# State-space phase with 1024-column scans and the step-times-B product of five of 16 states made on ScalarE

## Chip, core and metric

The kernel runs on one core of a Trainium2 chip. The metric is the device time of one launch in microseconds (us); lower is better. The engines are TensorE (PE, with its weight loads PEld), VectorE (DVE), ScalarE (ACT), GpSimd (POOL) and SyncE (SP, which here only issues DMAs).

## What is computed

Eight sequences of 512 tokens of width 128 pass through two blocks, each as `x = x + layernorm(block(layernorm(x)))`. The first block is a state-space layer (Mamba) in both directions, the second an attention and expert layer, which the change doesn't touch. Of the first block, for each direction (256 inner channels, 16 states):

```python
u = silu(conv(x @ Win_u) + convb)          # 4 taps, per channel
dtr, B, C = split(u @ Wx)                  # 8, 16 and 16 wide
dt = softplus(dtr @ Wdt + bdt)
def step(h, (dt_t, u_t, B_t, C_t)):        # over the 512 tokens
    h = exp(dt_t * A) * h + (dt_t * u_t) * B_t
    return h, sum_over_states(h * C_t)
y = (ys + u * D) * silu(x @ Win_z)
return y @ Wout                            # both directions and x are added
```

## The kernel before, in words

`mamba_phase` runs 16 units, one for each batch b and direction d, in the order (0,0), (0,1), (1,0) and so on. Channels lie on the partitions, in two halves h of 128; time lies along the columns. A unit has 32 steps s, one for each state n = s // 2 and half h = s % 2. In each step:

- ACT makes `da = exp(dt * A[n])` (`act_da`), 512 columns, up to 8 steps ahead of the scan that frees the buffer.
- PE broadcasts row n of B to all partitions with a 512-column bf16 product against a selection matrix (`pe_b`, L319), once for each state, into a PSUM bank.
- DVE multiplies it by `dtu = dt * u` (`dve_dbu`, L603) into another PSUM bank and runs the recurrence as one instruction (`dve_scan`, L610, a TENSOR_TENSOR_SCAN). It issues two products, then two scans.
- POOL multiplies the result by C[n], which lies broadcast in SBUF (`pool_hc`, L731).
- PE transposes each 128-column piece of that and adds it in PSUM (`pe_y`, L331), so that y is summed over the states with time on the partitions. It runs LAG_Y = 5 steps behind. The D term comes in the same way from `ud = u * D`, which ACT makes.

Beside the steps of one unit stands the preparation of the next, the *front*: layer norm (DVE, POOL), transposes `pe_xt` and copies `act_xpad` (only for direction 0), eight taps of the convolution `pe_u`, `act_silu_u`, `pe_z`, `act_silu_z`, then the table load back to exp and ln, `pe_xd`, `act_xd`, the split of B into three bf16 parts (`pool_rem`, `pool_part`), `pe_dt`, the softplus in four ACT steps a half (`act_soft`), `dve_dt`. And the *tail* of the unit before: `dve_yg`, `pe_ygt`, `act_ygt`, and behind direction 1 also `pe_out`, the second norm `dve_end` and `pool_x1`. PSUM is full: `bp` 2 banks, `dbu` 2, `yp` 2, `wp` 2; front and tail share `wp`.

The order of every engine's instructions is written out by hand: each of `pe_unit`, `act_unit`, `dve_unit` and `pool_unit` loops over the steps and says at which step of the current unit each piece of front or tail is issued. Each engine takes its instructions in that order, and a wait on a semaphore holds everything behind it. In the kernel before, PE issues the taps at s = 12 to 18, z at 19 and 20, xd at 21 and dt at 24 and 25; ACT issues silu and table load at s = 25, the xd copies at 27 and 30, the softplus at 31; DVE issues dt and dtu after scans 29 and 30, and res, the first step of `dve_end`, after scan 14. SP loads C for a whole unit with two broadcasts, of 1 and 3 MB, into a buffer with a place for each direction, and x right behind it.

## Time and profile before

| | us |
|---|---|
| median of 3 runs | 2225.64 (2219.59 to 2229.83) |
| the profiled execution, its own time | 2225.48 |
| its span, first to last instruction | 2223.7 |
| state-space phase within the span | about 0 to 1050 |

| engine | busy us (share of the span) |
|---|---|
| PE | 1614.2 (73%) |
| DVE | 1626.8 (73%) |
| ACT | 1174.6 (53%) |
| POOL | 1233.7 (55%) |

Busy time is the union of an engine's instructions; neighbours on one engine can overlap by a little, so the distance from start to start is the price of one in a dense stream, and the mean duration is somewhat more. The share over the whole span is a mean over two phases with different limits; the phase from 42 us (first unit) to about 1031 us (last scan) is the one that the change touches. A "granted clock" of 0.50 is TensorE at 1.2 GHz, 1.00 at 2.4 GHz.

### The profile page before, as it was taken

Reading aid. Unit: us, or ns where it says so; the run is one execution under the profiler, and the core shown is the slowest. Engines: PE = TensorE matmul, PEld = TensorE weight load, DVE = VectorE, ACT = ScalarE, POOL = GpSimd, SP = SyncE. Lnnn points to the kernel's source line nnn. Section 1 sums busy time; section 2 is a strip of 40 time slices with the busy share of each in tenths; the row PEclk is TensorE's granted clock in tenths of the full one; section 3 lists DMA queues with packets and bytes.
Section 4 is the critical chain, followed back from the end, with each engine's and each line's share of the span. In section 5 each row is a group of like instructions: output and inputs, shape, how many; then the busy total and the mean of one; then the engine's idle time right before and its main releaser. Section 6 shows DMA issues by size and latency. Waiting matters only on the chain.

```text
span 2223.7 us, 29267 instructions
## 1 busy us (share of the span) xinstructions
PE 1614.2 (73%) x7664; PEld 938.7 (42%) x7664; DVE 1626.8 (73%) x2538; ACT 1174.6 (53%) x1906; POOL 1233.7 (55%) x1097
## 2 busy tenths in 40 slices
PE   3677676766677666765376887877879888897888
PEld 1445454544455444544133343443434434343443
DVE  3999999999999999996262738456384654837455
ACT  4565555656565555561146391754727357282751
POOL 2777677777777677774336280643717346181541
PEclk8888777877888777775567598898989989899999
DMA  4212022121212011120301000000100001000000
GB/s 149 82 77 84 21 82 81 76 95 76 95 76 91 21 74 81 76 91 12 115 6 36 11 27 11 16 35 16 36 8 9 34 16 36 16 10 26 11 0 15
DMA packets 39620, 107.23 MB, mean 48 GB/s; under 512 B 4128, under 2 KB 30048, under 8 KB 34368
## 3 DMA queue, kind: packets, MB, share of 16 engines
q1 hardware_dynamic: 39520, 106.24, 12.6%
q14 instruction: 80, 0.66, 0.1%
q8 instruction: 20, 0.33, 0.1%
HBM read 92.99 MB, written 8.65 MB: 46 GB/s over the span
## 4 chain that ended last, share of the span: by engine, by line
issue 25%; POOL 13%; PE 6%; DVE 4%; DMA 2%; ACT 1%; SPq 0%; POOLq 0%; DVEq 0%; ACTq 0%
POOL pp L1892 9%; DMA k<-k_scratch 1%; DVE mx L1583 1%; PE pbk L1224 1%; PE po L1231 1%; PE pa L1218 1%; PE og L1167 1%; PE scores L1119 1%; PE scores L1117 1%; POOL ln_r L1822 0%; DVE rec L1611 0%; POOL kp L1855 0%; ACT pt L1414 0%; POOL rotk L1851 0%; PE scores L1147 0%
## 5 line engine op out<-in xcount | busy, mean ns | idle before, releaser
L731 POOL TENSOR_TENSOR hc<-hb,cb 128x512 f32<-128x512 f32 x512 | 653.8, 1295 | 249.3 <-DVE hb L610 221.4
L610 DVE TENSOR_TENSOR_SCAN hb<-da,dbu 128x512 f32<-128x512 f32 x512 | 599.5, 1202 | 5.6 <-DVE stats L635 4.0
L499 ACT ACTIVATE da<-dt,a_neg 128x512 f32<-128x512 f32 x512 | 351.9, 717 | 352.9 <-DVE hb L610 303.9
L331 PE MATMUL yp<-ident,hc 128*128 128x128 f32 x2048 | 359.0, 317 | 65.0 <-POOL hc L731 64.6
L1892 POOL TENSOR_TENSOR pp<-pt,pp 128x512 f16<-128x512 f32 x320 | 365.0, 1151 | 71.7 <-ACT pt L1414 71.3
L331 PEld LDWEIGHTS yp<-ident,hc 128*128 128x128 f32 x2048 | 297.9, 166 | 174.3 <-POOL hc L731 93.2
L603 DVE TENSOR_TENSOR dbu<-dtu,bp 128x512 f32<-128x512 f32 x512 | 323.8, 677 | 4.0 <-PE bp L319 3.2
L1583 DVE TENSOR_REDUCE mx<-scores 128x1 f32<-128x384 f32 (+3 forms) x352 | 218.4, 636 | 131.0 <-PE scores L1119 127.9
L1693 DVE SCALAR_TENSOR_TENSOR ga<-th,pa 128x512 f32<-128x512 f32 x128 | 87.6, 685 | 246.4 <-ACT th L1429 246.4
L1413 ACT ACTIVATE pp<-scores,lift 128x512 f16<-128x512 f32 x320 | 221.5, 692 | 46.3 <-PE scores L1147 45.4
L319 PE MATMUL bp<-st,sel 96*128 96x512 bf16 x256 | 116.4, 455 | 151.7 <-DVE dbu L603 149.0
L1414 ACT ACTIVATE pt<-scores,lift 128x512 f32<-128x512 f32 x320 | 222.1, 694 | 0.0
L1167 PE MATMUL og<-pp,vpad 128*128 128x512 f16 (+3 forms) x1024 | 192.7, 309 | 37.2 <-DVE osum L1603 28.4
L1117 PE MATMUL scores<-mask,identb 128*128 128x128 bf16 x512 | 116.9, 252 | 128.0 <-DVE mx L1583 68.3
L1429 ACT ACTIVATE th<-pa 128x512 f32<-128x512 f32 x128 | 77.1, 602 | 218.7 <-PE pa L1218 218.6
L1218 PE MATMUL pa<-h2t,w 128*128 128x512 f32 x256 | 157.8, 702 | 9.4 <-DVE ga L1693 9.0
L1119 PE MATMUL scores<-k,q 72*128 72x384 bf16 (+3 forms) x512 | 163.6, 362 | 0.0
L1167 PEld LDWEIGHTS og<-pp,vpad 128*128 128x128 bf16 x1024 | 96.4, 101 | 146.6 <-issue 46.8
L1117 PEld LDWEIGHTS scores<-mask,identb 128*128 128x128 bf16 x512 | 54.8, 110 | 241.2 <-DVE mx L1583 173.3
L1224 PE MATMUL pbk<-h2e,w 128*128 128x512 f32 x256 | 147.0, 658 | 12.0 <-DVE h2e L1687 10.8
L285 PE MATMUL wp<-xpad,wu 128*128 128x512 f32 x256 | 136.8, 627 | 21.8 <-ACT xpad L429 15.6
L1147 PE MATMUL scores<-q,k 75*128 75x512 bf16 (+3 forms) x512 | 141.1, 316 | 0.0
(181 smaller groups left out, 2265.6 us busy)
## 6 DMA issues: line engine op xcount, KB each, us to landing
cb<-c_scratch SPq DMA_DIRECT2D x16, 3072.0 KB, 11.8
cb<-c_scratch SPq DMA_DIRECT2D x16, 1024.0 KB, 4.6
q<-q_scratch SPq DMA_DIRECT2D x24, 288.0 KB
q_scratch<-qp SPq DMA_DIRECT2D x24, 128.0 KB
q<-q_scratch SPq DMA_DIRECT2D x24, 96.0 KB
xin<-in_x SPq DMA_DIRECT2D x8, 256.0 KB, 11.5
xres<-xin SPq DMA_DIRECT2D x8, 256.0 KB, 2.4
xres<-xln SPq DMA_DIRECT2D x8, 256.0 KB, 2.6
```

Of the source, the lines that this page charges most:

```text
L331: last = nc.tensor.matmul(yp[:, c, h * P:(h + 1) * P], src[:, c * P:(c + 1) * P], ident[:, :], is_transpose=True, start=(s < 0 and h == 0 ...
L499: nc.scalar.activation(da[:, s % NDA, :], dt[:, d, h, :], ACT.Exp, scale=a_neg[:, d, h, n:n + 1]).then_inc(da_done, 1)
L603: nc.vector.tensor_tensor(dbu[:, s % 2, :], dtu[:, d, h, :], bp[:, n % 2, :], ALU.mult).then_inc(dbu_done, 1)
L610: nc.vector.tensor_tensor_scan(hb[:, s % NHB, :], da[:, s % NDA, :], dbu[:, s % 2, :], 0.0, ALU.mult, ALU.add).then_inc(scan_done, 1)
L731: nc.gpsimd.tensor_tensor(hc[:, s % NHC, :], hb[:, s % NHB, :], cb[:, d, s // 2, :], ALU.mult).then_inc(hc_done, 1)
L1117: nc.tensor.matmul(sp_[:, t % 2, at + c * P:at + width], identb[:, :], mask[:, 0, :], start=(i == 0), stop=False, skip_group_check=True)
L1119: last = nc.tensor.matmul(sp_[:, t % 2, at:at + width], q9[0:PART_ROWS, h0_ + i, c * P:(c + 1) * P], k9[0:PART_ROWS, (h0_ + i) // 4, 0:width],
L1167: last = nc.tensor.matmul(og[:, kc * P:], vpad[:, kc, h, :], pp[:, t % NPR, part, at:at + SEQ - kc * P], start=first, stop=final, skip_gro ...
L1413: nc.scalar.activation(pp[:, t % NPR, 0, 0:width], scores_in, ACT.Exp, bias=lift[:, :], scale=SCALE)
L1414: nc.scalar.activation(pt[:, t % NPR, 0:width], scores_in, ACT.Exp, bias=lift[:, :], scale=SCALE).then_inc(exp_done, 1)
L1583: nc.vector.reduce_max(mx[:, c, h:h + n], sp_[:, t % 2, 0:n * (c + 1) * P].rearrange("p (n k) -> p n k", n=n), mybir.AxisListType.X).then_ ...
L1892: nc.gpsimd.tensor_tensor(pp[:, t % NPR, 1, 0:width], pt[:, t % NPR, 0:width], pp[:, t % NPR, 0, 0:width], ALU.subtract).then_inc(split_do ...
```

## The change

- A scan covers both halves: 1024 columns, with column 0 of each half of `da` held at zero, so that the second half starts afresh. `da`, `hb` and `hc` become 4 buffers of 1024 columns; `dbu` takes all four banks of `bp` and `dbu`.
- PE fills `dbu` directly (`pe_fill`), twice the B broadcast, and DVE multiplies in place, one product of 1024 columns, directly ahead of its scan.
- For states 3, 5, 7, 9 and 11 DVE makes no product. ACT multiplies in time-major layout, where B[n] is one number for each partition: `dbut = dtut * bt[n]`, four copies of 256 columns with a scale, and PE transposes it into `dbu` with eight transposes. For this the unit needs `dtut` (eight transposes of dtu at s = 1, one copy of 1024 columns at ACT's s = 5) and `bt` (eight products of 16 columns at s = 23, a small copy).
- The D term is a true product of u with a diagonal matrix (`diag_d`, made once) in place of ACT's `ud` and transposes.
- y runs 2 states behind. The front and tail steps move, as the diff shows.
- C lies in one buffer, loaded in four groups of 1 MB; x is loaded behind the kept copies.

```diff
+BY_ACT = (3, 5, 7, 9, 11)
+LAG_N = 2
-        cb = sb("cb", [P, NDIR, NS, SEQ])
+        cb = sb("cb", [P, NS, SEQ])
-        NDA, NHB, NHC = 8, 4, 8
+        NDA, NHB, NHC, NTB = 4, 4, 4, 3
...
+        def sp_batch(sp, b, last=False):
+            sp_c_write(sp, b + 1, 0)
+            for g in range(NGROUP):
+                sp_c_load(sp, b + 1, 0, g)
+            sp_c_write(sp, b + 1, 1)
+            for g in range(NGROUP - 1):
+                sp_c_load(sp, b + 1, 1, g)
+            sp_store(sp, b)
+            sp_keep(sp, b + 1)
+            if not last:
+                sp_x_load(sp, b + 2)
+            sp_c_load(sp, b + 1, 1, NGROUP - 1)
...
+        def pe_fill(pe, b, d, n):
+            pe.wait_ge(scan_done, count(scan_done, b, NS * d + n - 1))
+            if n in BY_DVE:
...
+                for h in range(NH2):
+                    last = nc.tensor.matmul(dbu[:, n % 2, h, :], sel[:, n, :], st[:, d, :], start=True, stop=True)
+            else:
+                pe.wait_ge(dbut_done, count(dbut_done, b, NA * d + BY_ACT.index(n) + 1))
+                for h in range(NH2):
+                    for c in range(TC):
+                        last = nc.tensor.transpose(dbu[:, n % 2, h, c * P:(c + 1) * P],
+                                                   dbut[:, BY_ACT.index(n) % NTB, c, h * P:(h + 1) * P], ident[:, :])
+            last.then_inc(b_ready, 1)
+
+        def pe_bt(pe, b, d):
+            pe.wait_ge(silu_done, count(silu_done, b, 4 * d + 4))
+            for c in range(TC):
+                for h in range(NH2):
+                    last = nc.tensor.matmul(wp[:, 1 - d, c * NS:(c + 1) * NS], u[:, h, c * P:(c + 1) * P],
+                                            wx[:, d, h, 0:NS], start=(h == 0), stop=(h == 1))
+            last.then_inc(bt_ready, 1)
...
+        def pe_front(pe, b, d, s):
+            if s == 13 and d == 0:
+                pe_xt(pe, b)
+            for i in range(NH2 * NTAP):
+                if s == (14, 15, 15, 16, 17, 18, 18, 19)[i] + 2 * (d == 0):
+                    pe_u(pe, b, d, i)
+            if s == 22:
+                pe_z(pe, b, d, 0)
+                pe_z(pe, b, d, 1)
+            if s == 23:
+                pe_xd(pe, b, d)
+                pe_bt(pe, b, d)
+            if s in (25, 26):
+                pe_dt(pe, b, d, s - 25)
...
             for s in range(STEPS):
+                n = s // 2
+                if s % 2 == 0:
+                    if n + 1 < NS:
+                        pe_fill(pe, b, d, n + 1)
+                    elif after:
+                        pe_fill(pe, *after, 0)
+                else:
+                    if n < LAG_N and tail:
+                        pe_y(pe, *tail, NS - LAG_N + n)
+                    if n == LAG_N + 1:
+                        for m in range(-1, n - LAG_N):
+                            pe_y(pe, b, d, m)
+                    if n > LAG_N:
+                        pe_y(pe, b, d, n - LAG_N)
+                if s == 1:
+                    pe_dtut(pe, b, d)
+                if tail and s == 8:
                     pe_ygt(pe, *tail)
+                if tail and tail[1] == 1 and s in (13, 14):
+                    pe_out(pe, tail[0], 2 * (s - 13))
+                    pe_out(pe, tail[0], 2 * (s - 13) + 1)
                 if front:
+                    pe_front(pe, *front, s)
...
+        def act_dbut(act, b, d, n):
...
+            for c in range(TC):
+                last = nc.scalar.activation(dbut[:, k % NTB, c, :], dtut[:, d, c, :], ACT.Copy,
+                                            scale=bt[:, d, c, n:n + 1])
+            last.then_inc(dbut_done, 1)
...
-            if at == 25:
+            if at == 23:
                 act_silu_u(act, b, d, 0)
                 act_silu_u(act, b, d, 1)
                 act_silu_z(act, b, d, 0)
                 act_silu_z(act, b, d, 1)
                 act.preload_act_table_set("natural_log_exp_and_others")
+            if at == 24:
+                act_xd(act, b, d, 0)
+                act_xd(act, b, d, 1)
+                act_bt(act, b, d)
+            if at == 26:
+                act_xd(act, b, d, 2)
+                act_xd(act, b, d, 3)
+            if at in (27, 28):
+                for k in range(4):
+                    act_soft(act, b, d, at - 27, k)
 
         def act_unit(act, b, d, front=None, tail=None):
             for s in range(STEPS):
                 act_da(act, b, d, s)
+                if s == 5:
+                    act_dtut(act, b, d)
+                if s % 2 == 1 and s // 2 + 1 in BY_ACT:
+                    act_dbut(act, b, d, s // 2 + 1)
+                if tail and s in (16, 17):
+                    act_ygt(act, *tail, s - 16)
                 if front:
                     act_front(act, *front, s)
...
+            for n in range(NS):
+                if n in BY_DVE:
+                    dve_dbu(dve, b, d, n)
...
+                dve_scan(dve, b, d, n)
+                if tail and n == LAG_N:
                     dve_yg(dve, *tail)
+                if tail and tail[1] == 1 and n in (9, 10, 11, 13):
+                    dve_end(dve, tail[0], {9: 0, 10: 1, 11: 2, 13: 3}[n])
...
+                if front and n == NS - 2:
+                    dve_dt(dve, *front, 0)
+                    dve_dt(dve, *front, 1)
```

## Rows read from the trace of the kernel before

**Rows 1.** Stretch, length; busy us of PE, PEld, DVE, ACT, POOL; clock, DMA, GB/s.
```profile
42.00:1000.00 958.00, 651.82 (x3192) 455.62 (x3193) 948.12 (x1238) 562.10 (x848) 692.16 (x565) 0.79 0.19 77
```

**Rows 2.** Groups by line and shape, 0 to 1090 us: busy, mean ns, idle before, releasers.
```profile
L610 DVE TENSOR_TENSOR_SCAN hb<-da,dbu 128x512 f32<-128x512 f32 x512 | 599.5, 1202 | 5.6 <-DVE stats L635 4.0 <-DVE stats L573 1.5
...
L603 DVE TENSOR_TENSOR dbu<-dtu,bp 128x512 f32<-128x512 f32 x512 | 323.8, 677 | 4.0 <-PE bp L319 3.2 <-DVE hb L610 0.6
```

**Rows 3.** DVE in order of time across a unit's border: start, us, line, operation.
```profile
534.63 1.54 DVE L590 TENSOR_TENSOR dt<-t_ln,t_relu 128x1024 f32<-128x1024 f32 x1
...
537.22 1.20 DVE L594 TENSOR_TENSOR dtu<-dt,u 128x1024 f32<-128x1024 f32 x1
538.33 1.21 DVE L610 TENSOR_TENSOR_SCAN hb<-da,dbu 128x512 f32<-128x512 f32 x1
539.46 1.26 DVE L603 TENSOR_TENSOR dbu<-dtu,bp 128x512 f32<-128x512 f32 x2
540.64 2.32 DVE L610 TENSOR_TENSOR_SCAN hb<-da,dbu 128x512 f32<-128x512 f32 x2
542.88 1.26 DVE L603 TENSOR_TENSOR dbu<-dtu,bp 128x512 f32<-128x512 f32 x2
...
596.61 1.53 DVE L590 TENSOR_TENSOR dt<-t_ln,t_relu 128x1024 f32<-128x1024 f32 x1
```

**Rows 4.** Waits by waiter and releaser, 0 to 1090 us: us, times, longest.
```profile
ACT da L499 <- DVE hb L610: 303.9, 266, 3.0
```

**Rows 5.** DVE in order of time at the start of the first unit.
```profile
42.33 1.22 DVE L590 TENSOR_TENSOR dt<-t_ln,t_relu 128x1024 f32<-128x1024 f32 x1 [25.03 <-ACT t_ln L487]
43.59 1.23 DVE L594 TENSOR_TENSOR dtu<-dt,u 128x1024 f32<-128x1024 f32 x1
```

**Rows 6.** PE in order of time where it is dense and at full clock.
```profile
561.63 0.38 PE L319 MATMUL bp<-st,sel 96*128 96x512 bf16 x1
561.85 0.60 PE L331 MATMUL yp<-ident,hc 128*128 128x128 f32 x4
562.28 1.06 PE L353 MATMUL wp<-wout,ygt 128*128 128x128 f32 x8
563.18 1.02 PE L285 MATMUL wp<-xpad,wu 128*128 128x512 f32 x2
564.04 0.60 PE L331 MATMUL yp<-ident,hc 128*128 128x128 f32 x4
```

**Rows 7.** PE in order of time, second phase: eight narrow fp32 instructions at full clock.
```profile
1364.05 0.95 PE L1194 MATMUL m<-gate,h2tn 128*128 128x8 f32 x8
```

**Rows 8.** ACT in order of time in the front of one unit.
```profile
579.00 0.60 ACT L449 ACTIVATE sz<-wp 128x512 f32<-128x512 f32 x1 [0.70 <-PE wp L294]
579.62 1.28 ACT L519 ACT_TABLE_LOAD   x1
580.92 1.34 ACT L499 ACTIVATE da<-dt,a_neg 128x512 f32<-128x512 f32 x2
582.16 0.57 ACT L457 ACTIVATE st<-wp 96x512 bf16<-96x512 f32 x1
...
588.52 0.66 ACT L479 ACTIVATE t_abs<-wp,col 128x512 f32<-128x512 f32 x1
...
590.97 0.69 ACT L479 ACTIVATE t_abs<-wp,col 128x512 f32<-128x512 f32 x1
```

**Rows 9.** PE in order of time from yg on.
```profile
549.94 1.94 PE L331 MATMUL yp<-ident,ud 128*128 128x128 f32 x8 [1.72 <-DVE yg L617]
```

**Rows 10.** Table of stretches around that burst; columns as in Rows 1.
```profile
548.00:552.00 4.00, 2.28 (x11) 2.09 (x11) 4.00 (x5) 1.44 (x2) 2.19 (x2) 0.50 0.00 0
552.00:556.00 4.00, 4.00 (x25) 3.94 (x24) 4.00 (x6) 1.58 (x3) 2.87 (x3) 0.65 0.00 0
556.00:560.00 4.00, 4.00 (x36) 3.82 (x35) 4.00 (x6) 2.17 (x4) 2.51 (x2) 1.00 0.00 0
```

**Rows 11.** DVE after the last scan of the phase.
```profile
1034.28 1.23 DVE L617 TENSOR_TENSOR yg<-yp,sz 128x1024 f32<-128x1024 f32 x1 [2.66 <-PE yp L331]
```

More of the change, by code:

```diff
@@ L75, in is_first @@
     return isinstance(b, int) and b == 0
+BY_ACT = (3, 5, 7, 9, 11)
+BY_DVE = tuple(n for n in range(NS) if n not in BY_ACT)
+NA, ND = len(BY_ACT), len(BY_DVE)
+NGROUP = 4
+PER_GROUP = NS // NGROUP
+LAG_N = 2
 def mamba_phase(nc, sems, x, x1, cscr, w):
@@ L133, in mamba_phase @@
         dtu = sb("dtu", [P, NDIR, NH2, SEQ])
-        ud = sb("ud", [P, NH2, SEQ])
-        cb = sb("cb", [P, NDIR, NS, SEQ])
+        diag_d = sb("diag_d", [P, NDIR, NH2, P])
+        dtut = sb("dtut", [P, NDIR, TC, DI])
+        bt = sb("bt", [P, NDIR, TC, NS])
+        cb = sb("cb", [P, NS, SEQ])
         yg = sb("yg", [P, TC, DI])
@@ new lines, in pe_bt, with pe_dtut @@
+        def pe_bt(pe, b, d):
[5 more added lines that the diff above has]
+            last.then_inc(bt_ready, 1)
+        def pe_dtut(pe, b, d):
+            pe.wait_ge(bt_done, count(bt_done, b, d + 1))
+            pe.wait_ge(soft_done, count(soft_done, b, 8 * d + 6))
+            pe.wait_ge(dt_done, count(dt_done, b, 2 * d + 2))
+            for c in range(TC):
+                for h in range(NH2):
+                    at = c % 2 * DI + h * P
+                    last = nc.tensor.transpose(wp[:, c // 2, at:at + P], dtu[:, d, h, c * P:(c + 1) * P], ident[:, :])
+            last.then_inc(dtut_ready, 1)
@@ L393, in pe_unit @@
             if not after:
-                for s in range(STEPS - LAG_Y, STEPS):
-                    pe_y(pe, b, d, s)
+                for n in range(NS - LAG_N, NS):
+                    pe_y(pe, b, d, n)
         @block.tensor
@@ L547, in _ @@
             nc.scalar.activation(sel[:, :, :], sel32, ACT.Copy).then_inc(sel_cast, 1)
-            for at in range(16, STEPS):
+            for d in range(NDIR):
+                for h in range(NH2):
+                    nc.scalar.activation(diag_d[:, d, h, :], ident[:, :], ACT.Copy,
+                                         scale=col[:, d, h, 2:3]).then_inc(diag_set, 1)
+            for at in range(STEPS):
                 act_front(act, 0, 0, at)
```

268 lines of the change are left out of this document (118 added, 150 removed).

## The prediction

> **What bounds the kernel now.** I read the table of stretches first [rows 1]. In the state-space phase, from 42 to 1000 us, DVE is busy 948 of 958 us, POOL 692, PE 652 and ACT 562; the change touches this phase alone. The groups by line and shape [rows 2] say what DVE does there: 512 scans of 1202 ns and 512 products dbu of 677 ns, with 5.6 and 4.0 us idle ahead of them. So DVE's own instruction stream is the clock of the phase. Its order in time [rows 3] gives the price that counts, start to start: two products and two scans (one state, both halves) take 542.88 - 539.46 = 3.42 us, of which the products take 1.18 and the scans 2.24. One scan takes 1.12 and not 1.20, because neighbours overlap. Two starts of dt lie 61.98 us apart: a unit is 62 us, of which 16 x 3.42 = 54.7 are states and 7.3 are dt, dtu, yg and the norm steps. ACT follows DVE: it waits 304 us for hb [rows 4], its largest wait, and PE follows in the same way. The slack there is what the change spends.
>
> **Part 1, wider DVE instructions.** A column of a scan costs 2 x 0.533 = 1.067 us per 512; 1.12 leaves 0.055 fixed. Scans of 1024 columns: 2 x 1.067 + 0.055 = 2.19 start to start. No row has such a scan; bounds are 2.13 and 2.24 (two of today's), and I take 2.19 since the 1024-column dtu starts its successor after 1.12, which is 1.067 + 0.055 [rows 3]. A 1024-column product alone is 1.12, but the scan now needs the product directly ahead of it; today another product lies between. A dependent neighbour shows at the start of the loop: dtu starts 1.26 after dt, which lasts 1.22 [rows 5]. With 1.20 for the steady product I take 1.23. A state whose product stays on DVE then costs 1.23 + 2.19 = 3.42: nothing gained (bounds 3.25 and 3.47, from the ends of both). That the product reads and writes the same PSUM bank no row shows; I price it as the 677 ns form scaled, with the scan's 2.24 as the far end.
>
> **Part 2, five states without a DVE product.** They cost 2.19 in place of 3.42. Per unit 11 x 3.42 + 5 x 2.19 = 48.6 against 54.7, a saving of 6.1; dtu now waits directly for dt (0.1) and I leave 0.3 for the tight product-scan pairs, so 5.7. Over 16 units **-91 us** if nothing stalls (bounds -78 and -133 by the ends above).
>
> Here a rule of the Trainium skill is worth weighing. The rows show a 1202 ns scan whose successor starts after 1.12 us, and 677 ns products 0.59 apart. The Trainium skill, "VectorE: DVE Perf Modes", section "The DRAIN you can't avoid", says that the next instruction does not start until the pipe is empty, and advises fewer instructions. By that rule the sum would be that of the first rival below; the trace does not agree with it.
>
> **Part 3, what goes to PE.** Prices at full clock, start to start [rows 6]: four transposes 0.44, a 512-column bf16 fill 0.22, eight halves of 128-column fp32 products 0.89, one tap of u 0.86 (two instructions of 512 columns, 0.43 each, so xd 1.72). Eight 8-column fp32 instructions last 0.95 [rows 7], so 0.11 each: narrow products are not cheaper. Per unit the fills go from 16 x 0.22 to 11 x 0.43 + 5 x 0.87 = +5.6; the transposed dtu +0.9; bt (8 products, 16 instructions) +1.8; the D term as true products against diag_d instead of transposes +0.9. About 33 us of full-clock work become 42, in a unit that should shrink to 56. In the mean it fits; the question is where it must be on time.
>
> **Part 4, what goes to ACT.** 20 copies of 256 columns (between 0.25 and 0.62, the da step back to back; I take 0.37), dtut 1.1, bt 0.3, less ud 1.3: +7.5 us, 36 of 62 busy becomes 43 of 56. Hidden except at the front, below.
>
> **Part 5, the front's schedule, which is the point.** PE reaches step s = 2n only when scan n - 1 has ended, because each fill waits for it. Write E10 for the end of scan 10. In the new order PE does z at s = 22, so after E10, xd and bt at 23; ACT does silu and the table load at 23, *between* da for state 11 and state 12, and xd and bt *between* the two halves of state 12. Today z is at s = 19 and 20 while ACT silus at 25 and copies xd at 27: then ACT already has da two states further. Chain after E10, from the rows of the front [rows 8] and PE's prices: fill 0.43, z 1.72 (eight fp32 instructions of 256 columns, 0.215 each, half of a tap's), result 0.2, silu 0.62, table load 1.30, da first half 0.62: 4.9. Copies st and xd 1.0: 5.9. Meanwhile PE does y 0.87, xd 1.72, bt 1.8, result 0.2: bt is there at 6.7, its copy ends at 7.0, and the second half of da at 7.7. DVE needs it after scan 11 and product 12, 2.19 + 1.23 = 3.4. **Stall 4.3 us**, with PE idle at E10. Queued behind the waiting bt copy on ACT is that da, and behind it on DVE scan 12.
>
> In units that prepare direction 0, PE is not idle at E10: between E7 and E10 (9.0 us) stand fills 9 to 11, y 6 to 8 and eight taps, 11.7 us. Backlog 2.6, stall 6.9. Then state 14. From there ACT has da 0.62, two copies 1.19, da 0.62, softplus of one half 2.45 [rows 8], da 0.62, softplus 2.45, da 0.72, together 8.7; DVE asks for the last after 2.19 + 3.42 + 1.23 = 6.8: stall 1.8. Together **8.7** in seven units.
>
> In units that prepare direction 1 behind another batch: the fifth tap of u, at s = 17, waits for res, which DVE now writes after scan 9; fill 10 stands behind that tap on PE, and DVE's next instruction is product 10. res 0.66, tap 0.86, fill 0.43, signals 0.2, less res itself 0.6: 1.5. Ahead of it, out, three taps, y and two fills (6.5 us) stand where DVE gives 5.6: 1.2. Then the front 4.3, the stall at 14 reduced to 0.5 by x1t. **7.5** in seven units. The first unit: 6.1. Sum 61 + 53 + 6 = **+120 us**.
>
> **Part 6, the rest.** The D term and y 0, 1 wait for yg and come in one burst at s = 7, ahead of fill 5. At the full clock 3.5 us, no stall; at half it ends 1.8 late. PE stands at half clock (0.50) ahead of yg now and rises within the burst [rows 9, 10]; I take 0.5 a unit, **+8** (0 to +29). The C rows come in four loads of 1 MB into one buffer instead of two; each group is free one unit ahead of its use, less its own 3 states, so hidden. x for the next batch is now loaded behind x_kept, after x1: I find it there 3 us before DVE asks; without that cover up to 3 us in seven units. After the last scan POOL and PE have a 1024-wide product and eight transposes, not 512 and four, **+1.6** [rows 11]. The start, ahead of the first dt at 42.3 [rows 5], is bound by the same PE and ACT steps; diag_d lies in ACT's wait for xt.
>
> Here the second rule of the Trainium skill. PE's burst from 549.94 on is all transposes until out at 556.9, but for one fill; the granted clock goes from 0.50 through 0.65 to 1.00 at 556 [rows 9, 10]. The Trainium skill, "TensorE: Matmul & The Clock Gate", section "Part 4: PE-mode transpose", says that transposes do not bring the full clock. By that rule the many new transposes would leave PE at 1.2 GHz and the burst would cost its 1.8 each time; the trace does not agree.
>
> **Sum.** -91 + 120 + 8 + 1.6 = +39 on the profiled execution's 2225.5 (span 2223.7 and 1.8 around it), which is also the median, 2225.6: **2264 us**. ACT's and PE's new waits take more than the removed products give.
>
> **Rivals.** (a) *DVE's fixed part is whole.* If each instruction paid its full duration (3.76 a state now), the saving were 60.1 - 11 x 3.47 - 5 x 2.27 = 10.6 a unit, 170 in all: 2225 - 170 + 130 = 2185. Against: rows 3. Chance 0.03. (b) *The order holds.* ACT and PE come through the front on time, DVE stays seamless: 2225 - 91 = 2135; some of the stalls stay: up to 2214. For: a third of PE's time and two fifths of ACT's are idle today [rows 1], and stalls let PE catch up. Against: the chain of 7.7 us against 3.4 is made of waits in the code. Chance 0.19. (c) *Only the bare front stalls*, 4.3 + 1.8 in 15 units, 92 us: 2227, no change. Chance 0.16. (d) *PE becomes the bound at half clock*: the 3.7 us wait for res, or the light stretch after the front, leaves it at 1.2 GHz when the taps come; eight taps, y and fills of 11.7 us would gain up to 3 us in each of 14 units, with the burst's 1.3 more: +40 to +60, 2305 to 2325. It decides once PE enters E7 at 0.5. Chance 0.09. (e) *The in-place product runs at the scan's rate*: 11 x 1.0 x 16 = +180, 2440. Chance 0.02. The forecast, 2240 to 2300: 0.51.
>
> **Chances.** 0.5% (about 11 us) is what a measurement here can tell from no change. Faster 0.22 (a, b); same 0.16 (c); slower 0.62. The range 2190 to 2300 leaves out most of (b) and (a) below, (d) and (e) above, 2 in 10.
>
> **What would show it.** Scans of about 2.27 us, products of 1.20, starts 3.42 apart in states 0 to 2 and 13; DVE idle before scan 12 and 14 with da as releaser, some 4 to 7 and 0.5 to 2 us a unit; idle before dbu 10 with a PE fill as releaser in every second unit; units of about 64 to 65 us. DVE idle under 3 us a unit would make the prediction wrong, and so would a scan above 2.3 us.

## The result, and the profile after

The changed kernel takes **2313.11 us** (median of 4, 2310.58 to 2320.85) against 2224.24 us for the kernel before beside it: ratio **1.0404**, interval 1.0368 to 1.044. It is slower, as forecast, but by 89 us and not by 39, above the range of 2190 to 2300.

I cut every profile at the same places. The *first phase* runs from the start of the first dt to the start of the last scan, the *second phase* (attention and experts, untouched) from the load of xa to the last instruction. All times are us of one profiled execution.

| | span | first phase | between | second phase |
|---|---|---|---|---|
| before | 2223.7 | 988.1 | 22.8 | 1170.4 |
| after | 2309.3 | 1101.7 | 25.6 | 1139.8 |
| difference | +85.6 | **+113.6** | +2.7 | **-30.6** |

So the first phase grew by three times what the forecast said, and a phase that the change doesn't touch gave some of it back. The table of stretches of the kernel after shows the first phase (columns as in [rows 1], where before stands):

```profile
42.00:1000.00 958.00, 691.20 (x3901) 528.02 (x3902) 821.79 (x602) 588.17 (x1026) 586.16 (x285) 0.84 0.18 67
```

DVE is no longer seamless: 822 of 958 us, where it was 948. Two views say where the time is. First the groups of DVE by line and shape, 0 to 1150 us, kernel after (busy, mean ns, idle before, releasers):

```profile
L710 DVE TENSOR_TENSOR_SCAN hb<-da,dbu 128x1024 f32<-128x1024 f32 x256 | 581.5, 2283 | 136.0 <-ACT da L591 78.6 <-DVE dbu L701 24.0 <-PE dbu L360 20.2
L701 DVE TENSOR_TENSOR dbu<-dtu,dbu 128x1024 f32<-128x1024 f32 x176 | 213.0, 1210 | 18.8 <-PE dbu L355 18.7
L694 DVE TENSOR_TENSOR dtu<-dt,u 128x1024 f32<-128x1024 f32 x16 | 48.9, 3059 | 1.8
L678 DVE TENSOR_SCALAR xln<-xin,mv,ln_r 128x128 f32<-128x128 f32 x32 | 23.5, 796 | 2.4 <-POOL ln_r L799 2.4
L678 DVE TENSOR_SCALAR xn<-xin,mv,ln_r 128x128 f32<-128x128 f32 x32 | 23.5, 794 | 0.0
```

and the same instructions in the kernel before, of which the prediction says nothing:

```profile
L594 DVE TENSOR_TENSOR dtu<-dt,u 128x1024 f32<-128x1024 f32 x16 | 19.1, 1195 | 0.0
...
L639 DVE TENSOR_SCALAR x1t<-res,mv,rstd 128x128 f32<-128x128 f32 x32 | 10.5, 389 | 1.4 <-POOL rstd L706 1.4
L578 DVE TENSOR_SCALAR xn<-xin,mv,ln_r 128x128 f32<-128x128 f32 x32 | 10.3, 383 | 0.0
L578 DVE TENSOR_SCALAR xln<-xin,mv,ln_r 128x128 f32<-128x128 f32 x32 | 9.5, 357 | 2.4 <-POOL ln_r L699 2.4
```

The scans and products have the durations that were forecast (2283 and 1210 ns). But dtu, the same instruction on the same data, went from 1.20 to 3.06 us, and the mean piece of xln, xn and x1t (the last steps of the two layer norms, four 128-column pieces each) doubled: +29.8, +14.0, +13.2 and about +13 us. These are *busy* us; a table of idle times doesn't show them. Second, DVE in order of time in the kernel after (start, us, line, operation, idle before):

```profile
522.35 1.20 DVE L690 TENSOR_TENSOR dt<-t_ln,t_relu 128x1024 f32<-128x1024 f32 x1
523.67 3.18 DVE L694 TENSOR_TENSOR dtu<-dt,u 128x1024 f32<-128x1024 f32 x1
...
576.01 1.23 DVE L701 TENSOR_TENSOR dbu<-dtu,dbu 128x1024 f32<-128x1024 f32 x1 [0.94 <-PE dbu L355]
582.97 2.29 DVE L710 TENSOR_TENSOR_SCAN hb<-da,dbu 128x1024 f32<-128x1024 f32 x1 [5.73 <-ACT da L591]
...
591.37 2.29 DVE L710 TENSOR_TENSOR_SCAN hb<-da,dbu 128x1024 f32<-128x1024 f32 x1 [1.39 <-POOL hc L829]
...
632.90 2.29 DVE L710 TENSOR_TENSOR_SCAN hb<-da,dbu 128x1024 f32<-128x1024 f32 x1 [1.47 <-PE dbu L360]
...
637.42 1.23 DVE L701 TENSOR_TENSOR dbu<-dtu,dbu 128x1024 f32<-128x1024 f32 x1 [1.65 <-PE dbu L355]
```

and POOL beside the first two of them:

```profile
522.59 3.17 POOL L829 TENSOR_TENSOR hc<-hb,cb 128x1024 f32<-128x1024 f32 x1 [2.43 <-DVE hb L710]
```

dt starts at 522.35; hc starts 0.24 later and takes 3.17 us instead of its usual 2.4; the extra 0.8 us fit a start that waits for dt's end at 523.55. Then dtu, directly behind dt, stands still until hc ends at 525.76: 525.76 - 523.67 + 1.1 = 3.2. dt has t_ln and t_relu in SBUF, dtu has dt and u, hc has hb and cb. Such a pair doesn't overlap: the one that comes second waits for the end of the other. The scans and products, with one operand in PSUM, do overlap with hc (none of the 256 scans takes more than 2.29 us, none of the 176 products more than 1.23). In the kernel before a scan lies between dt and dtu [rows 3], and hc has half the length; the same wait is there, but short (dt 1.54 us, one hc beside dtu 2.08 instead of 1.26).

The other part of the loss is idle time. These waits of DVE belong to the same phase (us, times, longest):

```profile
DVE hb L710 <- issue: 6.4, 2, 4.8
DVE hb L710 <- POOL hc L829: 4.2, 3, 1.4
```

By their place both are waits for da whose releaser the view names otherwise: the first are scans 12 and 14 of the first unit, the second are scan 14 in three of the seven units that prepare direction 0; in the other four the view names da for the same 1.39 us.

Account of the first phase. Scans and products: 16 x 54.7 = 875 before; after, 256 scans at 2.20 start to start, 154 products at 1.40 and 22 at 1.24 make 806: **-69**. Waits for POOL's instruction: 29.8 + 14.0 + 13.2 + 13, less 4.9 that dt gained: **+65**. Idle DVE: 78.6, 6.4 and 4.2 for da, 20.2 and 18.7 for fills are 128; less 9.6 in the same places before [rows 2]: **+118**. Together 114 of the 113.6 measured.

### The profile page after: what moved, and what is told of

Its sections match the earlier page's. It is cut to its first block and busy times, and to the rows that moved or that the text cites. A ratio compares the mean times of both kernels' runs of the same rounds, so it can differ in the third digit from the quotient of the medians.

```text
span 2309.3 us, 29961 instructions
## 1 busy us (share of the span) xinstructions
PE 1706.1 (74%) x8912; PEld 1067.2 (46%) x8912; DVE 1602.1 (69%) x1947; ACT 1280.5 (55%) x2230; POOL 1196.6 (52%) x841
## 3 DMA queue, kind: packets, MB, share of 16 engines
q1 hardware_dynamic: 44128, 106.24, 12.6%
## 5 line engine op out<-in xcount | busy, mean ns | idle before, releaser
L829 POOL TENSOR_TENSOR hc<-hb,cb 128x1024 f32<-128x1024 f32 x256 | 615.2, 2410 | 375.5 <-DVE hb L710 353.5
L710 DVE TENSOR_TENSOR_SCAN hb<-da,dbu 128x1024 f32<-128x1024 f32 x256 | 581.5, 2283 | 136.0 <-ACT da L591 78.6
L591 ACT ACTIVATE da<-dt,a_neg 128x511 f32<-128x511 f32 x512 | 334.8, 709 | 114.7 <-DVE hb L710 64.5
L398 PEld LDWEIGHTS yp<-ident,hc 128*128 128x128 f32 x2048 | 278.9, 159 | 68.4 <-issue 50.6
L398 PE MATMUL yp<-ident,hc 128*128 128x128 f32 x2048 | 306.2, 301 | 2.9 <-POOL hc L829 2.9
L355 PE MATMUL dbu<-st,sel 96*128 96x512 bf16 x352 | 127.7, 451 | 231.7 <-DVE hb L710 230.5
L701 DVE TENSOR_TENSOR dbu<-dtu,dbu 128x1024 f32<-128x1024 f32 x176 | 213.0, 1210 | 18.8 <-PE dbu L355 18.7
L355 PEld LDWEIGHTS dbu<-st,sel 96*128 96x128 bf16 x352 | 29.1, 108 | 280.2 <-DVE hb L710 200.2
L1316 PE MATMUL pa<-h2t,w 128*128 128x512 f32 x256 | 144.6, 648 | 4.0 <-DVE ga L1791 3.6
L360 PE MATMUL dbu<-ident,dbut 128*128 128x128 f32 x640 | 93.7, 294 | 61.6 <-DVE hb L710 53.7
```

Source lines behind the costliest of these rows:

```text
L398: last = nc.tensor.matmul(yp[:, c, h * P:(h + 1) * P], hc[:, n % NHC, h, c * P:(c + 1) * P], ident[:, :], is_transpose=True, start=False, ...
L591: nc.scalar.activation(da[:, n % NDA, h, 1:], dt[:, d, h, 1:], ACT.Exp, scale=a_neg[:, d, h, n:n + 1]).then_inc(da_done, 1)
L701: nc.vector.tensor_tensor(dbu[:, n % 2], dtu[:, d], dbu[:, n % 2], ALU.mult).then_inc(dbu_done, 1)
L710: nc.vector.tensor_tensor_scan(hb[:, n % NHB, :], da[:, n % NDA].rearrange("p h t -> p (h t)"), dbu[:, n % 2].rearrange("p h t -> p (h t)" ...
L829: nc.gpsimd.tensor_tensor(hc[:, n % NHC], hb[:, n % NHB, :].rearrange("p (h t) -> p h t", h=NH2), cb[:, n, :].unsqueeze(1).to_broadcast([P ...
```

## The experiments

Ratios are to the kernel before on the same chip, with 95% intervals. "Theory A" of the first is that DVE waits for the SBUF port that it shares with POOL.

**dtu one scan behind dt.**

```diff
-                if front and n == NS - 2:
-                    dve_dt(dve, *front, 0)
-                    dve_dt(dve, *front, 1)
+                if front and n >= NS - 2:
+                    dve_dt(dve, *front, n - (NS - 2))
```

> The changed kernel with one edit: DVE issues dt after scan 14 and dtu after scan 15, not one behind the other. In the changed kernel dtu lasts 3.18 us (1.20 before) and starts just after POOL has begun a 1024-column hc of 2.4 us. Theory A (a DVE instruction with two SBUF operands cannot run beside POOL's instruction and waits for its end; the length of POOL's instruction sets the wait): dtu goes first behind scan 15, lasts 1.20, and the phase from the first dt to the last scan falls from 1104 by 15 x 1.9 = 29 us, unless the later dtu delays something. Rival B (dtu is slow because it directly depends on dt, or because of the ACT steps that start on dt): B also speeds it up if the dependence is what costs, but then POOL's hc would not be lengthened; under A the hc that meets dt or dtu lasts 3.2 to 3.6 us. Rival C (nothing to do with neighbours): dtu stays at 3.2, no gain.

Measured 2282.71 us, ratio 1.0275 (1.0244 to 1.0307); first phase 1070.0, so -31.7. The group of dtu in this kernel:

```profile
L694 DVE TENSOR_TENSOR dtu<-dt,u 128x1024 f32<-128x1024 f32 x16 | 19.2, 1201 | 0.0
```

With a scan between, dtu takes 1.20 us again. It starts as that scan ends, before POOL has taken up the scan's hc, and now it is this hc that lasts 3.18 us. The 30 us were this wait, and a mere dependence of dtu on dt is ruled out.

**hc as two halves.**

```diff
-            nc.gpsimd.tensor_tensor(hc[:, n % NHC], hb[:, n % NHB, :].rearrange("p (h t) -> p h t", h=NH2),
-                                    cb[:, n, :].unsqueeze(1).to_broadcast([P, NH2, SEQ]), ALU.mult).then_inc(hc_done, 1)
+            for h in range(NH2):
+                last = nc.gpsimd.tensor_tensor(hc[:, n % NHC, h, :], hb[:, n % NHB, h * SEQ:(h + 1) * SEQ],
+                                               cb[:, n, :], ALU.mult)
+            last.then_inc(hc_done, 1)
```

> The changed kernel with one edit: POOL multiplies hc in two instructions of 512 columns instead of one of 1024; dt and dtu stay together. Theory A (the wait is for POOL's running instruction): dtu falls from 3.18 to about 2.1 (it waits for one instruction of 1.25), the longest of the norm steps x1t, xln, xn from 2.45 to about 1.3, each group of four from 3.2 to about 2.1; the phase falls by 15 x 1.1 + 22 x 1.1 = 41 us. Rival B (direct dependence of dtu on dt): dtu stays at 3.2, the norm steps too, and the phase changes by less than 5 us or grows, POOL having 256 more instructions.

Measured 2306.2 us, 1.0358 (1.0335 to 1.0381); first phase 1084.3, -17.4. Its groups:

```profile
L694 DVE TENSOR_TENSOR dtu<-dt,u 128x1024 f32<-128x1024 f32 x16 | 32.6, 2037 | 1.9
L678 DVE TENSOR_SCALAR xn<-xin,mv,ln_r 128x128 f32<-128x128 f32 x32 | 22.7, 770 | 0.0
```

dtu's wait shrinks with the length of POOL's instruction, so it is a wait for a whole instruction. The groups of four pieces keep their length: the piece that waited for the first half of hc gets in behind it, and the next one meets the second half (0.32, 1.36, 1.30 and 0.33 us in one group, where the whole hc gives 0.32, 2.45, 0.33 and 0.34). My expectation that they would return to those of before was wrong.

**xln spread over scans 7 to 10** (and xn, which PE waits for, made ahead of it).

```diff
-                if front and front[1] == 0 and n in (0, 1, 3, 4):
-                    dve_ln(dve, front[0], (0, 1, 3, 4).index(n))
+                if front and front[1] == 0 and n in (0, 1, 4):
+                    dve_ln(dve, front[0], (0, 1, 4).index(n))
+                if front and front[1] == 0 and 7 <= n < 7 + TC:
+                    dve_ln(dve, front[0], 3, (n - 7,))
```

> The changed kernel with one edit: xn is written first (after scan 4, as now) and the four pieces of xln one at a time behind scans 7 to 10. Theory A (a DVE instruction that needs the port that it shares with POOL waits for POOL's running one, and directly behind a scan it comes before POOL): of each group of four, three stand behind POOL's 2.4 us; alone behind a scan each piece lasts 0.34. xln falls from 23.5 us of busy time to about 11, the phase by 7 x 2 = 14 us. Rival (the norm steps are slow for another reason, as their scalar operands): 23.5 stays, no gain.

Measured 2289.28 us, 1.0301 (1.0279 to 1.0323); first phase 1077.5, -24.2.

```profile
L678 DVE TENSOR_SCALAR xln<-xin,mv,ln_r 128x128 f32<-128x128 f32 x32 | 11.5, 368 | 0.0
```

xln fell from 796 to 368 ns (23.5 to 11.5 us). Most of the other 12 us are shorter waits: the 6.9 us of product 12 for its fill are gone, scan 5 waits 8.5 instead of 10.8 and scan 12 72.9 instead of 74.1. (The view's da row falls further, 78.6 to 71.7, but only because it names hc for more of scan 14's unchanged waits.) A likely reason, not tested: behind scans 7 to 10 the pieces give PE time just ahead of the front, where four of them behind scan 3 gave none that was needed.

**The counts of the scan's waits computed ahead of the first.** In the kernel after a scan starts 1.40 behind its product in the loop, and 1.24 in the first and last unit, where the counts are constants. The edit does two things: the counts are computed ahead, and the wait for the product, which stood first, comes last.

```diff
+            da_now = count.in_register(dve, da_done, b, STEPS * d + 2 * n + 2)
+            hc_now = count.in_register(dve, hc_done, b, NS * d + n + 1 - NHB)
             if n in BY_DVE:
-                dve.wait_ge(dbu_done, count(dbu_done, b, ND * d + BY_DVE.index(n) + 1))
+                dbu_now = count.in_register(dve, dbu_done, b, ND * d + BY_DVE.index(n) + 1)
...
-            dve.wait_ge(da_done, count(da_done, b, STEPS * d + 2 * n + 2))
-            dve.wait_ge(hc_done, count(hc_done, b, NS * d + n + 1 - NHB))
+            dve.wait_ge(da_done, da_now)
+            dve.wait_ge(hc_done, hc_now)
+            dve.wait_ge(dbu_done if n in BY_DVE else b_ready, dbu_now)
```

> The changed kernel with one edit: in front of each scan all count values are computed first, and the wait for the product directly ahead comes last. In the changed kernel the scan starts 1.24 us behind its product in the first and last unit, whose counts are constants, and 1.40 in the loop, where they are worked out in registers. Theory: behind the wait that opens last stand two more register counts and waits on DVE's sequencer, 0.16 us for each of 154 pairs in the loop. Expected: pairs 1.40 to about 1.25 apart, 154 x 0.15 = 23 us less in the phase (from 1104), less what then waits for ACT or PE. Rival: the 0.16 is the register wait itself, whatever its place; then no change.

Measured 2337.19 us, 1.0505 (1.0488 to 1.0523). The spacing in the loop fell to 1.34 only, da's waits rose from 78.6 to 91.3, and the first phase became 6.1 us shorter, where 23 was expected. The total rose by 24, since the second phase took 1171.5. The last product and scan of the phase, in the last unit, kernel after and then this one:

```profile
1142.68 1.21 DVE L701 TENSOR_TENSOR dbu<-dtu,dbu 128x1024 f32<-128x1024 f32 x1
1143.92 2.29 DVE L710 TENSOR_TENSOR_SCAN hb<-da,dbu 128x1024 f32<-128x1024 f32 x1
```

```profile
1137.50 1.21 DVE L701 TENSOR_TENSOR dbu<-dtu,dbu 128x1024 f32<-128x1024 f32 x1
1138.84 2.29 DVE L713 TENSOR_TENSOR_SCAN hb<-da,dbu 128x1024 f32<-128x1024 f32 x1
```

Here the counts are constants in both, so that only the order of the waits differs, and the pair goes from 1.24 to 1.34 apart, as it does throughout the first and last unit. So the new order costs 0.10. If it costs that in the loop too, computing ahead gave back all of the 0.16 there, and the order took 0.10 of it again. A run with the counts ahead and the product's wait left first would show it; there is none.

**res after scan 8** in place of scan 9.

> The changed kernel with one edit: DVE writes res after scan 8, not 9, so the fifth tap of u on PE, and fill 10 behind it, no longer wait for scan 9. Theory of the prediction: the idle ahead of product 10 in seven units (1.65 us each, releaser a PE fill) goes, and PE starts the front up to 2 us earlier, 12 to 25 us less in the phase. Rival: PE is late anyway in that stretch (out and the taps), the idle moves to scan 10 or 11, less than 5 us.

Measured 2310.28 us, 1.0379 (1.0357 to 1.0401); first phase 1093.4, -8.3, where 12 to 25 was expected; the total is that of the kernel after within its noise. Product 10 waits 0.59 us for its fill instead of 1.65 in seven units (11.8 to 4.4 us in all), and scan 9 0.89 instead of 1.47, but scan 5 waits 3.7 us more. So the step with res behind the tap was there, and two thirds of its wait went.

**xd and bt copies behind both halves of da 12.**

```diff
-            if at == 24:
+            if at == 25:
                 act_xd(act, b, d, 0)
```

> The changed kernel with one edit: ACT copies st, xd and bt behind both halves of da for state 12 (s = 25) instead of between them (s = 24). Theory of the prediction: the idle before scan 12 (5.7 us in units that prepare direction 0, 4.2 in the others) is the chain z, silu, table load, da, copies, da; without the 1.0 us of copies and the 0.6 to 1.2 us of waiting for bt it shrinks by 1.8 to 2.5 us a unit, while softplus comes 0.6 later, so the idle before scan 14 grows by 0.6: the phase (first dt to last scan, 1102 us) falls by 15 x 1.5 = 22 us, bounds 10 and 35. Rival: dt and softplus are the chain that counts; then the idle before scan 14 grows by as much as the other shrinks and the phase stays within 5 us.

Measured 2311.56 us, 1.0407 (1.0379 to 1.0435); first phase 1090.8, -10.9, at the low end of the 10 to 35 expected; the total is unchanged. Waits for da: longest 3.8 instead of 5.7, but 46 in place of 31, 74.4 us in all. Scan 12 waits 44.9 us in place of 74.1; two thirds of that come back, 12.0 ahead of scan 13 and 8.4 ahead of scan 14.

**The front two steps earlier on PE**: z at s = 20, xd and bt at 21, dt at 24 and 25; taps and transposes come up to two steps earlier, out two steps, res and its norm two scans. On ACT ygt and xpad come earlier too, silu stays at s = 23, and the copies xd and bt go behind both halves of da, as in the run before.

```diff
-            if s == 22:
+            if s == 20:
                 pe_z(pe, b, d, 0)
                 pe_z(pe, b, d, 1)
-            if s == 23:
+            if s == 21:
                 pe_xd(pe, b, d)
                 pe_bt(pe, b, d)
...
-            if at == 24:
+            if at == 25:
                 act_xd(act, b, d, 0)
```

> The changed kernel with the order of the front and tail steps moved forward, nothing else: on PE out at s = 11 and 12, xt at 12, taps at 13 to 18 (14 to 19 for direction 0), z at 20, xd and bt at 21, dt at 24 and 25; on ACT ygt at 14 and 15, xpad at 16, the copies xd and bt at 25; on DVE res and the norm after scans 7, 8, 9, 11. Theory of the prediction: the 120 us of stalls come from the order alone. With z one state earlier the chain z, silu, table load, da ends 2 to 4 us earlier against DVE: the idle on da falls from 79 to under 15 us, that on PE fills from 39 to under 25, the phase from 1102 to about 1020 (bounds 1000 and 1045). Rival (PE is the bound: some 42 us of full-clock work in a unit of 57, with DVE's idle only moving from da to fills): the phase falls by less than 30 us and PE fills take over as releaser.

Measured 2283.34 us, 1.0254 (1.023 to 1.0279); first phase 1067.1, -34.6, where 1020 was expected. That is nearer to the rival (less than 30, fills take over as releaser). DVE's waits in this kernel:

```profile
DVE dbu L701 <- PE dbu L355: 53.2, 30, 4.0
...
DVE hb L710 <- PE dbu L360: 18.7, 16, 1.7
DVE hb L710 <- ACT da L591: 15.1, 14, 2.0
```

The waits for da fell by 63.5 us as intended, and those for fills rose by 33. PE in order of time shows why:

```profile
557.81 1.89 PE L327 MATMUL wp<-win_z,xpad 128*128 128x256 f32 x8
559.53 1.04 PE L398 MATMUL yp<-ident,hc 128*128 128x128 f32 x8
560.41 1.88 PE L336 MATMUL wp<-u,wx 128*128 128x512 f32 x4
562.13 1.85 PE L369 MATMUL wp<-wx,u 128*128 128x16 f32 x16
563.83 0.59 PE L355 MATMUL dbu<-st,sel 96*128 96x512 bf16 x2
```

Fill 12 stands behind z, xd and bt; the product waits 4.01 us for it in seven units and 3.33 in one, 31.4 of the 53.2 us. Product 10 waits in all 15 units now, and product 8 in seven.

**xd and bt behind fill 12** (s = 22), else the same.

> e7_front_early left 72 us of DVE waiting for a fill of dbu, because fill 12 stood on PE behind z, xd and bt. Here xd and bt go behind fill 12 (s = 22 in place of 21), all else as in e7. Theory A (PE's order, not its total load, made those waits): fill 12 comes 1.72 + 1.85 us earlier in 15 units, idle before dbu with a fill as releaser from 53 to about 20 us, the waits for da back to 20 to 30 us since bt comes 1 us later than in e7; first phase 1067 to about 1040 (bounds 1025 to 1055). Rival B (PE is simply full there, at full clock): what is moved behind fill 12 stalls fill 13 instead, first phase stays at 1060 to 1070.

Measured 2282.84 us, 1.0286 (1.0243 to 1.033); first phase 1067.0, the same to 0.1 us. Waits for L355 fell from 53.2 to 29.6, those for da rose from 15.1 to 39.3, of which 33.5 stand ahead of scan 14: bt comes later by the fill, and what ACT has queued behind its copy with it. Rival B holds for the time, but only in small part for its mechanism: fill 13 was late by 0.5 us in eight units (4 us), the rest is da. Between these two runs the order says only for which engine DVE waits.

**All repairs together**: that order, dtu apart, and xln and x1t spread over four scans.

> The order of e9, dtu one scan behind dt (e1), xln and x1t spread over four scans each in place of groups of four (e6). Theory A (the waits for the shared port and the waits in the front are separate and add): from the first phase of e9 take 32 for dtu, 24 for xln and about 15 for x1t: 1040 - 71 = about 970 us, which would be less than the 988 of the kernel before, and with a second phase of 1140 to 1170 a total of 2180 to 2215. Rival B (they are bound to each other: DVE time given back is lost again as waits for PE and ACT, since these set the pace): first phase 1010 to 1040, total 2220 to 2270, no better than before.

Measured 2218.77 us (median of 10), 0.9983 (0.9967 to 0.9999); first phase 1006.7. The 970 expected had started from 1040 for e9, which took 1067.0. From there it lost 60.3 of the 71 that the waits add up to, so they are separate losses. The rest is a new wait:

```profile
DVE stats L673 <- DMA xin<-in_x: 12.6, 7, 2.5
```

2.5 of it lies ahead of the first unit, as in every kernel here; the other 10 us are six waits for x, which is loaded behind the store of x1, and x1 had moved from behind scan 12 in e9 to scan 15.

**The same with the counts ahead.**

> e10 with the counts of the scan's three waits computed ahead of the first wait (e3). In e3 this took 6 us off the first phase and the total rose by 24 since the second phase, which is the same code, took 1171.5 us in place of 1140. Theory A: first phase 6 to 10 us under e10's. For the second phase I have no theory; if the edit itself slows it, it is 20 to 30 us over e10's, if e3's was a chance of its timing, both lie anywhere between 1139 and 1172.

Measured 2240.09 us, 1.0072 (1.0055 to 1.0089); first phase 1004.5, -2.2 where 6 to 10 was expected; second phase 1164.3 in place of 1143.9. Twice now this edit went with a second phase 20 to 32 us longer.

**xn spread too, its transposes one step later, x1 one state earlier.**

> e10 with the last group of four on DVE, xn, also spread, one piece behind each of scans 3 to 6 (and the transposes of xn one step later, at s = 13), and with x1t and x1 one state earlier, so that the load of x behind x1's store lands before DVE asks for it. Theory A (each wait for the port and for x is a loss of its own): xn from 23.5 to 11.5 us, DVE's idle before the statistics from 12.6 to 2 us, so the first phase from 1006.7 to about 984 (bounds 975 to 995), below the 988 of the kernel before; total 2190 to 2205 with a second phase near 1140. Rival B (DVE is now paced by da and the fills, and time given back returns as their waits): first phase 995 to 1007, waits for da and fills up from 80 us by what was saved, total 2208 to 2220.

Measured 2234.94 us, 1.0041 (1.0025 to 1.0057); first phase 1016.5, *longer* by 9.8, though both waits went (xn 23.5 to 10.2 us, the wait for x 12.6 to 2.5). Neither theory allowed that. DVE's waits, ACT's wait for the moved transposes, and the stretches around one of them (columns as in [rows 1]):

```profile
DVE hb L710 <- ACT da L591: 62.0, 51, 2.9
...
ACT xpad L504 <- PE wp L301: 32.3, 7, 4.6
```

```profile
516.00:520.00 4.00, 1.75 (x13) 1.01 (x10) 4.00 (x3) 0.66 (x1) 2.51 (x2) 0.99 0.00 0
520.00:524.00 4.00, 3.15 (x9) 2.02 (x10) 3.81 (x4) 4.00 (x9) 3.07 (x2) 0.50 0.00 0
524.00:528.00 4.00, 4.00 (x15) 2.53 (x15) 1.09 (x3) 4.00 (x9) 2.36 (x1) 0.66 0.00 0
```

PE waits for the last piece of xn behind scan 6, ACT waits 4.6 us for the transposes with da queued behind the copy, and the granted clock falls from 0.99 to 0.50 after PE's idle stretch, just as the taps come. Scan 9 then waits 2.9 us for da, in seven units.

**x1 one state earlier alone** (xn a group of four again, transposes at s = 12).

> e10 with x1t behind scans 10 to 13 in place of 11 to 14 and x1 ahead of hc 14 in place of hc 15, so that x1's store and the load of x behind it come one state earlier; xn stays a group of four, and the transposes of xn stay at s = 12. Theory A (e12 lost through its later transposes, which held ACT's copy and the da behind it): DVE's idle before the statistics from 12.6 to 2.5 us, waits for da stay at 45 to 50, first phase 1006.7 to about 997 (bounds 992 to 1003). Rival B (what is given back returns as waits for da and fills, whichever way): first phase stays at 1004 to 1010. Total 997 + 51 + 1140 to 1160 + 20, so 2205 to 2228.

Measured **2200.59 us** (6 runs, 2198.19 to 2208.58), ratio **0.991** (0.9892 to 0.9927); first phase 992.6.

```profile
DVE hb L710 <- ACT da L591: 44.3, 44, 2.5
...
ACT xpad L504 <- PE wp L301: 20.8, 7, 3.1
```

Theory A holds: the 10 us for x came back whole here, where no PE or ACT step moved. It fits the reading of the run before it. This version is 0.9% faster than the kernel before, but look where: its first phase is 4.5 us *longer* than that of the kernel before (988.1), its second, of the same code, 27.7 shorter (1142.7 against 1170.4). As far as these runs show, the change with its repairs gains nothing in the phase it is made in; open are the 13 us that xn's group of four still waits for POOL and the 35 us ahead of scan 14.

**The second phase.** Three runs only delay its start, by repeating the last store of x1 with a wait each: once in the kernel before (2.4 us), and eight times in both kernels (18.9 and 18.6 us).

```diff
             sp_store(sp, NB - 1)
             sp.wait_ge(x1_stored, count(x1_stored, NB - 1, 16))
+            sp_store(sp, NB - 1)
+            sp.wait_ge(x1_stored, count(x1_stored, NB - 1, 32))
```

> The kernel BEFORE with one edit: at the end of the first phase the last store of x1 is issued and waited for a second time, which delays the start of the second phase by 2 to 3 us and changes nothing in it. In the changed kernel and its variants the untouched second phase takes between 1139.6 and 1171.5 us, with the granted clock going from 0.89 to 0.94 with it; before it takes 1170.4. Theory: how the second phase falls against TensorE's clock depends on when it begins, not on what the first phase did; then a mere delay moves the second phase too, by up to 30 us either way. Rival: something in the first phase (PE work, buffers) sets it; then the second phase stays at 1170 within 3 us and the whole is 2 to 3 us longer.

Measured 2226.83 us, 1.0007 (0.9994 to 1.002), 3.7 over the kernel before; second phase 1166.2, in an execution 5.4 us under that median.

> The kernel before, with the store of x1 of the last batch repeated eight times, each awaited, so that all engines stand idle 8 x 2.5 to 2.7 = some 20 us longer between the two phases; nothing else differs. Theory A (the second phase depends on when it starts, or on the idle stretch ahead of it): its length moves from 1170 towards 1140, total 2224 + 21 - 20 to 30 = 2215 to 2225. Rival B (it does not): 1166 to 1171 again, total 2224 + 21 = 2245 (bounds 2241 to 2248).

Measured 2239.53 us, 1.0085 (1.0068 to 1.0102): 18.2 over the kernel before, which is the delay. The profiled execution, 3.6 us under that median, had a second phase of 1162.2.

> The same delay in the changed kernel. Theory A: the second phase leaves 1140 and takes 1150 to 1171, total 2313 + 21 + 10 to 30 = 2345 to 2365. Rival B: 1137 to 1142, total 2313 + 21 = 2334 (bounds 2330 to 2338).

Measured 2336.16 us, 1.0507 (1.0487 to 1.0526): 23 over the kernel after; second phase 1148.4. In the profiled executions both phases move by some 8 us towards each other, but those of the kernel before and its variants lie up to 5.4 us beside their medians. By the medians, less the delay, the second phase moved by +1, -1 and +4 to +5 us. A later start or a longer idle stretch is not what makes the 30 us.

## Why the prediction was right in sign and wrong in size

- **Part 1, the wider scan and product**: right. 2283 and 1210 ns; 2.20 start to start for the scan (2.19 taken). The dependent pair was taken as 1.23 from [rows 5], at the very start, where counts are constants. In the loop it is 1.40: `<-DVE dbu L701 24.0` above, 122 times 0.2. The upper end of the bounds for a state, 3.47, was too low: it is 3.60.
- **Part 2**: -91 became -69, mostly for that reason (154 x 0.16 = 25), which is outside the bounds of -78 and -133: the end of -78 held a pair price from a place without counts to compute, and that of -133 none at all. Rival (a) stays refuted: scans of 2.29 us that follow each other take 4.46 for two. The section that the prediction weighs for it, "The DRAIN you can't avoid" of the Trainium skill's "VectorE: DVE Perf Modes", adds that a next instruction that is not held starts earlier; with that sentence the trace agrees.
- **The step that failed** is one that was not written as a step: dt, dtu, yg and the norm steps were kept at their old price. The text of part 2 even says "dtu now waits directly for dt (0.1)". It cost 1.86 a unit, and with the norm groups **65 us**, more than the whole miss of 49. The mechanism was in reach: [rows 3] show a dt of 1.54 us where [rows 5], ahead of POOL's first hc, show 1.22. Two equal instructions of different length on one engine ask for an explanation. The Trainium skill states the rule: "GPSIMD Engine Reference", section "1. Specifications", says that POOL's SBUF interfaces are shared with VectorE and contended by DVE instructions with two SBUF inputs. Also in the Trainium skill, "SBUF — State Buffer", section "Who interferes with whom", calls the shared port pair an exclusive lock. The trace agrees, with 3.18 against 1.20 us.
- **Parts 3 and 5, the front**: right, and close. Forecast 120 + 8 of new DVE idle time, measured 118 net. (In its term of 1.2 the prediction's own numbers, 6.5 less 5.6, give 0.9.) The chain after E10 is there step by step on ACT, kernel after:

```profile
578.35 1.28 ACT L610 ACT_TABLE_LOAD   x1
579.65 0.72 ACT L591 ACTIVATE da<-dt,a_neg 128x511 f32<-128x511 f32 x1
580.41 0.59 ACT L529 ACTIVATE st<-wp 96x512 bf16<-96x512 f32 x1
580.90 0.58 ACT L534 ACTIVATE xd<-wp 128x512 f32<-128x512 f32 x1
582.10 0.22 ACT L564 ACTIVATE bt<-wp 128x64 f32<-128x64 f32 x1 [0.61 <-PE wp L369]
582.22 1.32 ACT L591 ACTIVATE da<-dt,a_neg 128x511 f32<-128x511 f32 x2
...
590.63 1.93 ACT L591 ACTIVATE da<-dt,a_neg 128x511 f32<-128x511 f32 x3
```

  bt stands between the halves of da, and scan 12 waits 5.73 us, with 0.94 ahead of product 12 (6.9 forecast in these units, 4.3 in the others, where 4.16 is measured). Scan 14: 1.39 for 1.8; the profile puts it down to hc, but the da that begins at 590.63 and takes 0.7 ends right ahead of the scan's start at 591.37. Product 10: 1.65 for 1.5. Fill 9: 1.47 for 1.2.
- **Part 4**: 20 copies of 256 columns last 495 ns each and 1.69 for four, 0.40 from start to start; 0.37 was taken. Hidden.
- **Part 6**: the burst for yg is there below full clock (the D term takes 3.1 to 3.8 us), and scan 5 waits behind it from not at all to 2.2 us, 10.8 in all, where 0.5 a unit, 8, was taken. The end cost 2.7 for 1.6. C and x loads were hidden.
- **The untouched phase** was taken at its old time, and took 30.6 less. No view of before could tell that, and it is luck: without it the forecast would have missed by some 80 us.
- A unit (dt to dt, 522.35 to 593.57) takes 71.2 us where 64 to 65 was forecast; behind the first (57.2) they take 69.0 to 71.4. The total missed by 49: +22 in part 2, +65 for the waits for POOL, -10 on idle time (118 for 128), +1 at the end, -31 in the second phase, together +47; the rest is the distance of one execution from the median.
- **The sign** came from the front, and that holds without the missed step: 113.6 less 65 leaves a first phase 49 us longer, of which the waits for da and fills are more than the whole. With the second phase as it came out that would be some 20 us, 1% slower: the sign would have held, but narrowly.
- **The rivals**: the time lies in the range of (d), 2305 to 2325, but not for its reason. The granted clock of the first phase is 0.84, above the 0.79 of before, and the taps that (d) would have at half clock run at full, 0.43 us from start to start, in all 15 units that have them:

```profile
571.92 1.88 PE L318 MATMUL wp<-xpad,wu 128*128 128x512 f32 x4
```

  (d)'s mechanism showed only in an experiment of mine, e12, where a moved step let PE stand idle ahead of the taps.

## What to carry to other kernels

An instruction that the change does not touch can still change its price: when POOL's instructions become twice as long, list every DVE instruction with both operands in SBUF (and fp32 tensor_scalar) and ask what POOL runs beside it; one such instruction directly behind a scan is cheap, a second directly behind the first waits for the whole of POOL's. When a chain over two engines has little slack, moving steps gives back a part and changes who is waited for (e5 gave 11 us of the 22 expected, e7 35 of 82, e9 nothing); find a step that has slack, or take time off the bound engine where no partner's order moves (e1, e10, e15). And take the price of a dependent pair from the middle of the loop, with the waits in the order in which the kernel will have them.

## What the runs showed that I had not expected

- A tensor_scalar of 128x128 on SBUF waits for POOL as an instruction with two SBUF operands does: four in a row 1.11 us alone (ahead of the first unit) and 3.20 beside a 2.4-us hc, spread singly 0.33 to 0.37 each in the mean.
- A scan starts 0.03 us behind the end of the product ahead of it where the wait counts are constants, 0.19 where they are computed in the loop, and 0.13 in both places when the wait for the product comes last of three and the counts are computed ahead.
- The second phase, of equal code, took from 1139.5 to 1171.5 us. The stretches of before and after, columns as in [rows 1]:

```profile
1053.00:2223.00 1170.00, 914.32 (x4304) 451.54 (x4304) 637.03 (x1232) 585.95 (x1022) 509.62 (x498) 0.85 0.07 24
```

```profile
1169.00:2309.00 1140.00, 881.85 (x4304) 438.59 (x4304) 644.71 (x1232) 585.25 (x1022) 509.27 (x498) 0.88 0.07 24
```

  The same 4304 instructions keep PE busy 32 us less, at a granted clock of 0.88 in place of 0.85. It goes with the kernel and is not a chance of one execution, as the medians follow it (e3 is 24 us slower than after with a shorter first phase). Three delays of its start moved it by 5 us at most, by the medians. What sets it stays open, and so a difference of 1% between two kernels of this program need not lie in the part that was changed.
